# Tile 4's mask and eviction, two bank copies and four loads take other places in their engines' queues

## The chip, the cores and the metric

One core of a Trainium2 chip runs the whole kernel. The metric is the device time of one execution in microseconds (us). The kernel before takes 1176.93 us, the median of 3 runs (1176.62 to 1178.44).

## The reference

A transformer block with modulation, over 1024 tokens of width 512: a layernorm scaled and shifted, causal attention (32 query heads of size 128, which share 8 key and value heads, with rotary embedding), a gated residual, a second layernorm, and a dense layer with a low-rank part whose rank a router chooses per token. All in float32.

```python
q = (x @ wq).reshape(B, T, H, HD).transpose(0, 2, 1, 3)
k = (x @ wk).reshape(B, T, KV, HD).transpose(0, 2, 1, 3)
v = (x @ wv).reshape(B, T, KV, HD).transpose(0, 2, 1, 3)
q = q * cos + _rotate_half(q) * sin
k = k * cos + _rotate_half(k) * sin
...
scores = jnp.where(mask, scores, -jnp.inf)
att = jax.nn.softmax(scores, axis=-1)
out = jnp.einsum('bhts,bhsd->bhtd', att, v)
out = out.transpose(0, 2, 1, 3).reshape(B, T, H * HD)
return out @ wo
...
x = x + ga * _L0_attn_ref(h, L0_attn_wq, L0_attn_wk, L0_attn_wv, L0_attn_wo)
h = _layernorm(x, axis=-1) * (1 + cb) + sb
x = x + gb * _L0_ffn_ref(h, L0_ffn_W, L0_ffn_b, L0_ffn_A, L0_ffn_B, L0_ffn_gate_w, L0_ffn_gate_b)
```

## The kernel before, in words

Every float32 operand of a matmul is split into a high and a low part, and each product is three matmuls (high by high, high by low, low by high). ScalarE (ACT) writes the high part as a copy, VectorE (DVE) the low part as a subtraction: `split_hi` and `split_lo` for weights, `transposed_hi` and `transposed_lo` for probabilities, `rotated_hi` and `rotated_lo` for q and k, `output_hi` and `output_lo` for the attention output, `early_hi` and `early_lo` for the early probabilities (`pa_hi`, `pa_lo`).

The work runs over 8 groups of 4 heads (R = 4, one key and value head per group). A head is a `front` and a `back`, and every engine has its own list of both, written out by hand; semaphores tie the lists together. The next group's q, k and v are projected in the `back` of head 3, and the output projection of the group before (`wo`, tiles 0 to 7) lies in heads 0 and 1 of the next one. Which projection lies where is in `fillers(h, place, first)`: places 1 to 5 of a head, on TensorE (PE) and in the queues of the engines that evict it.

The scores of a head are 8 row tiles. Tile i has 128(i+1) keys. `masked` (DVE) adds the mask and takes the maximum, `exp` is ACT's, `inverse` (DVE) is the reciprocal of the row sum, `normalise` is GpSimd's (POOL). Tiles 0 to 3 are turned by DVE (`turn`), go to DRAM as `p_rows` and come back as `pa_lo` (`turn_columns`, SyncE's queue); tiles 4 to 7 are transposed on PE (L602) into 2 banks named `transposed`, and evicted as `pb_hi` (ACT) and `pb_lo` (DVE). PE may write a bank again once the subtraction of its last content is done. Two banks named `accumulators` hold projections and the products with v (`pva` for tokens 0 to 511, `pvb` for the rest): a bank is free when `a_taken` counts its eviction, which for q and k is `times_cos` (DVE, behind ACT's `swap_halves`, L926 and L927), for v `copy_values`. Then POOL's `rotate` multiplies by the sine (L1536) and adds (L1540).

Weights come over SyncE's queue into `stage`, which has 2 slots used in turn. A load waits until the weight two numbers before it has been split by DVE (`w_lo`); `w_number` gives each weight its number and so its slot. The `wo` weights are scaled on POOL (`scale_wo`, L1546) before their split. In the last group the weight W of the dense layer is loaded into `trig`, the table of the rotary embedding, once the last q has been rotated.

Of the kernel before, what the change touches and what calls it, by code (L numbers as in the profile page):

```python
# [22 lines left out]
P = 128  # L23
# [5 lines left out]
GROUPS = KV_HEADS  # L29
# [243 lines left out]
def adaln_block(nc, x, wq, wk, wv, wo, ffn_w, ffn_b, ffn_a, ffn_bb, gate_w, gate_b, c, wmod, out):  # L273
# [7 lines left out]
    with ExitStack() as ctx:  # L281
# [150 lines left out]
        W_GROUP = [("q", 1), ("q", 2), ("wo", 0), ("q", 3), ("wo", 1), ("wo", 2), ("wo", 3)]  # L432
        W_NEXT = [("q", 0), ("k", 0), ("v", 0)]
        W_PER = len(W_GROUP) + len(W_NEXT)

        def w_number(what, at, ahead=0):

            if what in W_GROUP:
                base = len(W_FIRST) + W_GROUP.index(what) + 1 + W_PER * (at.g + ahead)
            elif at.g + ahead == 0:  # L440
                base = W_FIRST.index(what) + 1
            else:
                base = len(W_FIRST) + len(W_GROUP) + W_NEXT.index(what) + 1 + W_PER * (at.g + ahead - 1)
# [37 lines left out]
        def _(sp):  # L481
# [58 lines left out]
            for g in range(GROUPS):  # L540
# [19 lines left out]
            sp.wait_ge(r_sum, N.value("r", ("q", (3, 1)), G7))  # L560
            sp.wait_ge(a_taken, N.value("a", ("q", (3, 1)), G7))
            sp.dma_start(fw_in, ffn_w.rearrange("(o p) i -> p o i", p=P)).then_inc(f_in, 16)
# [325 lines left out]
        def _(act):  # L888
# [74 lines left out]
            def front(h, at):  # L963
# [16 lines left out]
                else:  # L980
                    split_hi(("wo", 3), at)
# [93 lines left out]
            exp(3, 4, G7)  # L1075
            weight_hi(("W", 0), fw_hi[:, 0, :])
            exp(3, 5, G7)
# [69 lines left out]
        def _(dve):  # L1147
# [155 lines left out]
            def front(h, at):  # L1303
                hb, ahead = before(h, at)
                masked(h, 0, at)
# [358 lines left out]
```

## Time and profile before

| | |
|---|---|
| median of 3 runs | 1176.93 us |
| the profiled execution's own time | 1176.61 us |
| its span (first to last instruction) | 1174.8 us |
| mean granted TensorE clock, share of full | 0.987 |
| PE busy | 1059.3 us (90%) |
| PE weight loads busy | 875.7 us (75%) |
| DVE busy | 782.9 us (67%) |
| ACT busy | 633.2 us (54%) |
| POOL busy | 513.5 us (44%) |
| DMA, mean | 68 GB/s |

The busy times are of one execution, 1.8 us of which lie outside the span. PE is the engine that is nearly always busy, and the difference between its busy time and the span, 115.5 us, is what its idle stretches add up to. The views that follow give each such stretch with the instruction that ended it. The low part of v's weight, which stands once in each group, starts at 36.1 us and for the eighth time at 951.1; in the middle of the kernel one group follows the other after some 133 us, and head 2 takes some 23 of them.

### The profile page before, as it was taken

The page shows a single profiled execution, that of the slowest core. Times are in us where ns is not written, and L with a number is a line of the kernel's source. Part 1 is how long each engine was busy: PE and PEld are TensorE (multiplying, and loading weights), DVE is VectorE, ACT ScalarE, POOL GpSimd, SP SyncE. Part 2 cuts the span into 40 slices and gives each one's busy share as a digit, 9 for nine tenths or more (in the row PEclk, how much of TensorE's full clock was granted, in tenths as well). Part 3 has the DMA queues.
Part 4 walks back from the last instruction along what each step waited for, and adds up shares of the span by engine and source line. Part 5 has one row for each costly group of instructions (what it writes and reads, how often), then busy time and mean ns, then how long its engine had stood idle before and what let it go on. Part 6 is the DMA issues. An engine that isn't in the chain of part 4 may idle for free.

```text
span 1174.8 us, 16608 instructions
## 1 busy us (share of the span) xinstructions
PE 1059.3 (90%) x5480; PEld 875.7 (75%) x5480; DVE 782.9 (67%) x1842; ACT 633.2 (54%) x1306; POOL 513.5 (44%) x506
## 2 busy tenths in 40 slices
PE   6999889998999889998999989998999989994898
PEld 3678778786878778786878768786878768784776
DVE  4668765686558765587548766587548856584576
ACT  6446753575346753476337754476337654473443
POOL 2525642465225642356225543356325643353234
PEclk8999999999999999999999999999999999997999
DMA  6352301222102401223102311123102311123001
GB/s 216 119 179 95 104 19 54 63 73 81 54 1 73 120 24 55 63 64 90 54 1 69 111 38 54 50 77 90 55 1 63 104 49 55 46 80 99 1 19 55
DMA packets 61118, 79.84 MB, mean 68 GB/s; under 512 B 5669, under 2 KB 46757, under 8 KB 60905
## 3 DMA queue, kind: packets, MB, share of 16 engines
q1 hardware_dynamic: 61032, 78.77, 21.9%
q8 instruction: 45, 0.74, 0.3%
q14 instruction: 41, 0.33, 0.1%
HBM read 55.69 MB, written 23.07 MB: 67 GB/s over the span
## 4 chain that ended last, share of the span: by engine, by line
PE 67%; ACT 12%; DVE 11%; issue 5%; POOL 2%; DMA 2%; SPq 1%; POOLq 0%; DVEq 0%; ACTq 0%
PE accumulators L629 18%; PE accumulators L659 15%; PE accumulators L644 15%; PE scores L589 9%; PE transposed L602 6%; ACT qr L927 2%; ACT qr L926 2%; DVE p_large L1169 2%; ACT p_large L892 2%; DVE pb_lo L1181 2%; ACT pb_hi L900 2%; PE scores L857 2%; DVE turned L1193 2%; POOL qc L1540 1%; ACT o_hi L917 1%
## 5 line engine op out<-in xcount | busy, mean ns | idle before, releaser
L1527 POOL TENSOR_SCALAR p_large<-p_large,rowinv 128x640 f32<-128x640 f32 (+3 forms) x128 | 125.8, 983 | 243.5 <-DVE rowinv L1174 243.5
L1181 DVE TENSOR_TENSOR pb_lo<-transposed,pb_hi 128x512 fp32r<-128x512 f32 (+3 forms) x256 | 138.7, 583 | 104.5 <-ACT pb_hi L900 104.5
L1536 POOL TENSOR_TENSOR qr<-qr,trig 128x512 f32<-128x512 f32 x80 | 103.4, 1293 | 229.9 <-ACT qr L927 229.9
L892 ACT ACTIVATE p_large<-p_large,negmax 128x640 f32<-128x640 f32 (+3 forms) x128 | 126.5, 988 | 140.0 <-DVE negmax L1169 140.0
L900 ACT ACTIVATE pb_hi<-transposed 128x512 fp32r<-128x512 f32 (+3 forms) x256 | 117.5, 510 | 145.5 <-PE transposed L602 143.8
L602 PE MATMUL transposed<-ident,p_large 128*128 128x128 f32 x832 | 114.3, 276 | 36.3 <-DVE pb_lo L1181 29.6
L589 PE MATMUL scores<-k_hi,q_hi 128*128 128x512 f32 (+2 forms) x384 | 140.6, 366 | 0.0
L602 PEld LDWEIGHTS transposed<-ident,p_large 128*128 128x128 f32 x832 | 95.5, 141 | 60.2 <-issue 39.3
L1540 POOL TENSOR_TENSOR qc<-qc,qr 128x512 f32<-128x512 f32 x80 | 108.6, 1358 | 63.3 <-DVE qc L1223 60.7
L1169 DVE CUSTOM_DVE_ANT_0 p_large<-scores,mask 128x640 f32<-128x640 f32 (+3 forms) x128 | 128.2, 1010 | 5.8 <-PE scores L589 4.5
L589 PE MATMUL scores<-k_hi,q_lo 128*128 128x512 f32 (+2 forms) x384 | 132.0, 344 | 0.0
L589 PE MATMUL scores<-k_lo,q_hi 128*128 128x512 f32 (+2 forms) x384 | 131.5, 342 | 0.0
L1527 POOL TENSOR_SCALAR p_small<-p_small,rowinv 128x128 f32<-128x128 f32 (+3 forms) x128 | 97.4, 779 | 62.9 <-DVE rowinv L1174 62.5
L926 ACT ACTIVATE qr<-accumulators 64x512 f32<-64x512 f32 x80 | 47.7, 596 | 111.1 <-PE accumulators L644 109.7
L1248 DVE TENSOR_TENSOR y<-accumulators,y 128x512 f32<-128x512 f32 x64 | 44.1, 689 | 86.8 <-PE accumulators L659 86.8
L659 PE MATMUL accumulators<-wo_hi,o_hi 128*128 128x512 f32 x256 | 70.6, 397 | 11.1 <-DVE qc L1223 9.2
L644 PE MATMUL accumulators<-h_hi,wq_hi 128*128 128x512 f32 x256 | 70.0, 395 | 11.6 <-DVE wq_lo L1260 11.2
L589 PEld LDWEIGHTS scores<-k_hi,q_lo 128*128 128x128 f32 x384 | 72.6, 189 | 6.9
L1223 DVE TENSOR_TENSOR qc<-accumulators,trig 128x512 f32<-128x512 f32 x80 | 54.9, 686 | 34.1 <-ACT qr L927 34.0
L589 PEld LDWEIGHTS scores<-k_hi,q_hi 128*128 128x128 f32 x384 | 72.8, 190 | 5.9 <-issue 0.9
L589 PEld LDWEIGHTS scores<-k_lo,q_hi 128*128 128x128 f32 x384 | 73.2, 191 | 5.1
L1169 DVE CUSTOM_DVE_ANT_0 p_small<-scores,mask 128x128 f32<-128x128 f32 (+3 forms) x128 | 61.7, 486 | 20.6 <-PE scores L589 19.0
(167 smaller groups left out, 2278.2 us busy)
## 6 DMA issues: line engine op xcount, KB each, us to landing
p_rows<-turned SPq DMA_DIRECT2D x32, 640.0 KB, 2.9
pa_lo<-p_rows SPq DMA_DIRECT2D x128, 160.0 KB, 3.2
stage<-in_L_attn_wq_dram SPq DMA_DIRECT2D x32, 256.0 KB, 2.8
stage<-in_L_attn_wo_dram SPq DMA_DIRECT2D x32, 256.0 KB, 3.5
y<-in_L_wmod_dram SPq DMA_DIRECT2D x4, 512.0 KB, 5.7
stage<-in_L_attn_wk_dram SPq DMA_DIRECT2D x8, 256.0 KB, 2.8
stage<-in_L_attn_wv_dram SPq DMA_DIRECT2D x8, 256.0 KB, 3.8
y<-in_L_wmod_dram SPq DMA_DIRECT2D x1, 2048.0 KB, 10.6
```

Source lines behind the costliest of these rows:

```text
L589: mm = nc.tensor.matmul(S_flat[:, c0 + key:c0 + key + n], a[:, i * P:(i + 1) * P], b[:, key:key + n], start=(k == 0), stop=(k == 2))
L602: mm = nc.tensor.transpose(TB[:, b, (j % 4) * P:(j % 4 + 1) * P], row(i)[:, j * P:(j + 1) * P], ident[:])
L629: mm = nc.tensor.matmul(acc[:, c0:HALF], v[:, j, :], pt, start=(hi and v is v_hi and j == 0), stop=(not hi and j == 4 * half + 3))
L644: mm = nc.tensor.matmul(acc, a[:, k, :], b[:, k, half * HALF:(half + 1) * HALF], start=(n == 0), stop=(n == 3 * KC - 1))
L659: mm = nc.tensor.matmul(acc, a[:, r, t * P:(t + 1) * P], b[:, r, :], start=(n == 0), stop=(n == 3 * R - 1))
L892: nc.scalar.activation(row(i), row(i), ACT.Exp, bias=negmax[:, i:i + 1], scale=-1.0, accum_out=rowsum[:, i:i + 1]).then_inc(s_exp, 1)
L900: nc.scalar.activation(pt_of(i, part, True), src, ACT.Copy).then_inc(t_hi, 1)
L1169: nc.vector.tensor_tensor_reduce(row(i), S_flat[:, c0:c0 + n], mask[:, T - n:T], -SCALE, 3.4e38, ALU.add, ALU.min, negmax[:, i:i + 1]).the ...
L1181: nc.vector.tensor_tensor(pt_of(i, part, False), src, f32(pt_of(i, part, True)), ALU.subtract).then_inc(t_lo, 1)
L1527: nc.gpsimd.tensor_scalar(row(i), row(i), rowinv[:, i:i + 1], 1.0, ALU.mult, ALU.mult).then_inc(s_norm, 1)
L1536: nc.gpsimd.tensor_tensor(qr[:, s, :], qr[:, s, :], trig[:, 1, half * HALF:(half + 1) * HALF], ALU.mult).then_inc(r_sin, 1)
L1540: nc.gpsimd.tensor_tensor(qc[:, s, :], qc[:, s, :], qr[:, s, :], ALU.add).then_inc(r_sum, 1)
```

## The change

No operation is added or taken away; PE's list is the same row by row. The lists of the other four queues are:

- `masked(h, 4)` (DVE) goes from the start of `back` to the end of `front`, ahead of `turn` of tile 3.
- `transposed_hi` of tile 4 (ACT) goes ahead of the `swap_halves` of place 4.
- The `wo` 0 and `wo` 1 splits go behind that.
- The last bank copy of a head's place 5 (`times_cos` of q, or `copy_values` of the second half of v) goes ahead of masks 0 and 1 of the next `front` (DVE).
- The split of the next group's first q goes from the `back` of head 3 to its `front`, and takes the place of the split of `wo` 3; that one, with its scaling, goes into the `back`, behind tile 4's eviction. Their loads and numbers change places too.
- The split of v goes ahead of the early probabilities.
- The load of W goes ahead of the last head's `turn_columns`.

```diff
-        W_GROUP = [("q", 1), ("q", 2), ("wo", 0), ("q", 3), ("wo", 1), ("wo", 2), ("wo", 3)]
-        W_NEXT = [("q", 0), ("k", 0), ("v", 0)]
+        W_GROUP = [("q", 1), ("q", 2), ("wo", 0), ("q", 3), ("wo", 1), ("wo", 2)]
+        W_LATE = [("q", 0), ("wo", 3), ("k", 0), ("v", 0)]
...
@@ SyncE
                 turn_columns(R * g + 2)
-                load(("wo", 3), at)
                 if g + 1 < GROUPS:
                     load(("q", 0), at, 1)
+                    load(("wo", 3), at)
                     load(("k", 0), at, 1)
+                else:
+                    load(("wo", 3), at)
+                    sp.wait_ge(r_sum, N.value("r", ("q", (3, 1)), G7))
+                    sp.wait_ge(a_taken, N.value("a", ("q", (3, 1)), G7))
+                    sp.dma_start(fw_in, ffn_w.rearrange("(o p) i -> p o i", p=P)).then_inc(f_in, 16)
                 turn_columns(R * g + 3)
...
@@ ScalarE: front, then back
-                else:
-                    split_hi(("wo", 3), at)
+                elif at.g + 1 < GROUPS:
+                    split_hi(("q", 0), at, 1)
...
-                if last:
-                    split_hi(("q", 0), at, 1)
                 exp(h, 4, at)
                 exp(h, 5, at)
+                transposed_hi(h, 4, at)
+                fill(h, 4, at)
                 if h == 1:
                     split_hi(("wo", 0), at)
                 if h == 2:
                     split_hi(("wo", 1), at)
-                fill(h, 4, at)
-                transposed_hi(h, 4, at)
                 if last:
+                    split_hi(("wo", 3), at)
                     split_hi(("k", 0), at, 1)
                 exp(h, 6, at)
                 transposed_hi(h, 5, at)
                 rotated_hi(("q", ((h + 1) % R, 0)), at, int(last))
+                if last:
+                    split_hi(("v", 0), at, 1)
                 early_hi(h, at)
...
-                fill(h, 5, at, slice(0, 1) if last else slice(0, -1))
-                if last:
-                    split_hi(("v", 0), at, 1)
-                    fill(h, 5, at, slice(1, -1))
+                fill(h, 5, at, slice(0, -1))
...
@@ VectorE: front, then back
+                if h or not at.first:
+                    fill(hb, 5, at, slice(-1, None), -ahead)
                 masked(h, 0, at)
                 masked(h, 1, at)
                 if h or not at.first:
-                    fill(hb, 5, at, slice(-1, None), -ahead)
                     output_lo(hb, 0, at, ahead)
...
+                masked(h, 4, at)
                 turn(h, at, 3)
...
-                masked(h, 4, at)
                 fill(h, 2, at)
-                if last:
-                    split_lo(("q", 0), at, 1)
                 masked(h, 5, at)
...
                 fill(h, 4, at, slice(-1, None))
+                if h == 1:
+                    split_lo(("wo", 0), at)
+                if h == 2:
+                    split_lo(("wo", 1), at)
                 if last:
+                    split_lo(("wo", 3), at)
                     split_lo(("k", 0), at, 1)
...
@@ GpSimd: from front to back
-                if h == R - 1:
-                    scale_wo(3, at)
                 normalise(h, 0, at)
...
                 normalise(h, 5, at)
                 if h == 2:
                     scale_wo(2, at)
+                if last:
+                    scale_wo(3, at)
                 rotate(("q", ((h + 1) % R, 0)), at, int(last))
...
@@ the last head (tail), VectorE
-            masked(3, 4, G7)
-            weight_lo(("W", 0), 1, fw_hi[:, 0, :], fw_lo[:, 0, :])
             inverse(3, 4, G7)
             masked(3, 5, G7)
+            inverse(3, 5, G7)
+            split_lo(("wo", 3), G7)
+            weight_lo(("W", 0), 1, fw_hi[:, 0, :], fw_lo[:, 0, :])
             weight_lo(("W", 1), 2, fw_hi[:, 1, :], fw_lo[:, 1, :])
-            inverse(3, 5, G7)
             transposed_lo(3, 4, G7)
```

ScalarE in the `back` of a head 3, from the exponentials of tiles 4 and 5 to the split of k's weight, before: L926 and L927 are `swap_halves`, L900 is `transposed_hi`.

```order
L892 ACTIVATE p_large,rowsum<-p_large,negmax 128x640
L892 ACTIVATE p_large,rowsum<-p_large,negmax 128x768
L926 ACTIVATE qr<-accumulators 64x512
L927 ACTIVATE qr<-accumulators 64x512
L900 ACTIVATE pb_hi<-transposed 128x4x128
L900 ACTIVATE pb_hi<-transposed 128x128
L956 ACTIVATE wk_hi<-stage 128x512
```

The same stretch after:

```order
L896 ACTIVATE p_large,rowsum<-p_large,negmax 128x640
L896 ACTIVATE p_large,rowsum<-p_large,negmax 128x768
L904 ACTIVATE pb_hi<-transposed 128x4x128
L904 ACTIVATE pb_hi<-transposed 128x128
L930 ACTIVATE qr<-accumulators 64x512
L931 ACTIVATE qr<-accumulators 64x512
L960 ACTIVATE wo_hi<-stage 128x512
L960 ACTIVATE wk_hi<-stage 128x512
```

Tile 4's two evictions stand ahead of the swap, and `wo` 3's split has come in behind it.

ScalarE a little further on in the same head, from the evictions of tile 5 on, before: `q_hi` is `rotated_hi`, `pa_hi` is `early_hi`, the row with 1024 columns is the exponential of tile 7.

```order
L900 ACTIVATE pb_hi<-transposed 128x4x128
L900 ACTIVATE pb_hi<-transposed 128x2x128
L935 ACTIVATE q_hi<-qc 128x512
L906 ACTIVATE pa_hi<-pa_lo 128x4x320
L892 ACTIVATE p_large,rowsum<-p_large,negmax 128x1024
L926 ACTIVATE qr<-accumulators 64x512
L927 ACTIVATE qr<-accumulators 64x512
L956 ACTIVATE wv_hi<-stage 128x512
```

The same stretch after:

```order
L904 ACTIVATE pb_hi<-transposed 128x4x128
L904 ACTIVATE pb_hi<-transposed 128x2x128
L939 ACTIVATE q_hi<-qc 128x512
L960 ACTIVATE wv_hi<-stage 128x512
L910 ACTIVATE pa_hi<-pa_lo 128x4x320
L896 ACTIVATE p_large,rowsum<-p_large,negmax 128x1024
L930 ACTIVATE qr<-accumulators 64x512
L931 ACTIVATE qr<-accumulators 64x512
```

The split of v's weight stands ahead of `pa_hi`, of tile 7's exponential and of k's swap, where it stood behind them.

SyncE's loads from the `wo` 1 and 2 weights of a group to v of the next one, before:

```order
L506 DMA stage<-in_L_attn_wo_dram 128x512 x2
L513 DMA p_rows<-turned 128x1280
L519 DMA pa_lo<-p_rows 32x4x320 x4
L506 DMA stage<-in_L_attn_wo_dram 128x512
L506 DMA stage<-in_L_attn_wq_dram 128x4x128
L506 DMA stage<-in_L_attn_wk_dram 128x4x128
L513 DMA p_rows<-turned 128x1280
L519 DMA pa_lo<-p_rows 32x4x320 x4
L506 DMA stage<-in_L_attn_wv_dram 128x4x128
```

The same after:

```order
L508 DMA stage<-in_L_attn_wo_dram 128x512 x2
L515 DMA p_rows<-turned 128x1280
L521 DMA pa_lo<-p_rows 32x4x320 x4
L508 DMA stage<-in_L_attn_wq_dram 128x4x128
L508 DMA stage<-in_L_attn_wo_dram 128x512
L508 DMA stage<-in_L_attn_wk_dram 128x4x128
L515 DMA p_rows<-turned 128x1280
L521 DMA pa_lo<-p_rows 32x4x320 x4
L508 DMA stage<-in_L_attn_wv_dram 128x4x128
```

The loads of the first q and of `wo` 3 change places; v's load stands where it stood, but by its number it waits for the split of `wo` 3 and no longer for that of q.

## Rows read from the trace of the kernel before

**Rows 1.** The page's chain that ended last, whole span: share by engine.
```profile
PE 67%; ACT 12%; DVE 11%; issue 5%; POOL 2%; DMA 2%; SPq 1%; POOLq 0%; DVEq 0%; ACTq 0%
```

**Rows 2.** TensorE's waits: who, for whom, us in total, times, longest.
```profile
PE transposed L602 <- DVE pb_lo L1181: 29.6, 31, 1.0
PE accumulators L644 <- DVE wv_lo L1260: 13.9, 7, 2.0
PE accumulators L789 <- DMA trig<-in_L_ffn_W_dram: 13.3, 1, 13.3
PE accumulators L644 <- DVE wq_lo L1260: 11.2, 7, 1.6
PE accumulators L644 <- DVE vt L1239: 9.3, 7, 1.5
PE accumulators L659 <- DVE qc L1223: 9.2, 7, 1.3
PE transposed L602 <- POOL p_large L1527: 6.7, 17, 1.6
...
PE accumulators L644 <- DVE wk_lo L1260: 1.2, 7, 0.2
```

**Rows 3.** Timeline of TensorE, 640 to 690: start, us, operation, idle before.
```profile
649.93 0.77 PE L602 MATMUL transposed<-ident,p_large 128*128 128x128 f32 x5 [0.31 <-POOL p_large L1527]
...
652.89 0.84 PE L602 MATMUL transposed<-ident,p_large 128*128 128x128 f32 x6 [0.98 <-DVE pb_lo L1181]
...
671.60 1.16 PE L644 MATMUL accumulators<-h_hi,wq_hi 128*128 128x512 f32 x4 [1.60 <-DVE wq_lo L1260]
...
687.40 1.16 PE L644 MATMUL accumulators<-h_hi,wv_hi 128*128 128x512 f32 x4 [1.99 <-DVE wv_lo L1260]
```

**Rows 4.** Timeline of ScalarE, 650 to 685.
```profile
651.42 0.77 ACT L900 ACTIVATE pb_hi<-transposed 128x512 fp32r<-128x512 f32 x2
...
681.29 1.26 ACT L906 ACTIVATE pa_hi<-pa_lo 128x1280 fp32r<-128x1280 f32 x1
...
682.45 1.14 ACT L892 ACTIVATE p_large<-p_large,negmax 128x1024 f32<-128x1024 f32 x1
...
683.71 0.60 ACT L926 ACTIVATE qr<-accumulators 64x512 f32<-64x512 f32 x1
```

**Rows 5.** Timeline of VectorE, 650 to 687.
```profile
652.05 0.89 DVE L1181 TENSOR_TENSOR pb_lo<-transposed,pb_hi 128x512 fp32r<-128x512 f32 x2 [0.55 <-ACT pb_hi L900]
...
678.90 0.68 DVE L1260 TENSOR_TENSOR wk_lo<-stage,wk_hi 128x512 fp32r<-128x512 f32 x1
...
685.59 1.67 DVE L1260 TENSOR_TENSOR wv_lo<-stage,wv_hi 128x512 fp32r<-128x512 f32 x1
```

**Rows 6.** GpSimd: timeline at 685, and line 1546 (min/median/max ns).
```profile
685.44 1.27 POOL L1536 TENSOR_TENSOR qr<-qr,trig 128x512 f32<-128x512 f32 x1
...
L1546 POOL TENSOR_TENSOR stage<-stage,ga_b x32: 1286/1298/1718, 90.5 to 1062.7; 128x512 f32<-128x512 f32 x32
```

**Rows 7.** SyncE's issue at 674, its landing; all loads into stage (min/median/max).
```profile
674.93 0.43 SPq L506 DMA_DIRECT2D stage<-in_L_attn_wv_dram  x1
...
stage<-in_L_attn_wv_dram SPq DMA_DIRECT2D x1, 256.0 KB, 3.7
...
DMA to landing us min/median/max: 2.5/2.9/10.5
```

**Rows 8.** The tail: timelines of TensorE and GpSimd, and the W load's landing.
```profile
1081.74 1.97 PE L789 MATMUL accumulators<-ident,trig 128*128 128x128 f32 x8 [13.33 <-DMA trig<-in_L_ffn_W_dram]
...
1099.24 1.20 PE L659 MATMUL accumulators<-wo_hi,o_hi 128*128 128x512 f32 x4 [1.96 <-DVE o_lo L1215]
...
1061.45 1.29 POOL L1540 TENSOR_TENSOR qc<-qc,qr 128x512 f32<-128x512 f32 x1
...
trig<-in_L_ffn_W_dram SPq DMA_DIRECT2D x1, 1024.0 KB, 8.2
```

**Rows 9.** Busy by stretch: PE, PEld, DVE, ACT, POOL, PEclk, DMA share, GB/s.
```profile
1080.00:1090.00 10.00, 6.63 (x31) 5.85 (x32) 4.04 (x9) 3.35 (x8) 1.71 (x2) 0.56 0.12 40
```

More of the change, by code:

```diff
@@ L431, in adaln_block @@
         W_FIRST = [("k", 0), ("q", 0), ("v", 0)]
-        W_GROUP = [("q", 1), ("q", 2), ("wo", 0), ("q", 3), ("wo", 1), ("wo", 2), ("wo", 3)]
-        W_NEXT = [("q", 0), ("k", 0), ("v", 0)]
-        W_PER = len(W_GROUP) + len(W_NEXT)
+        W_GROUP = [("q", 1), ("q", 2), ("wo", 0), ("q", 3), ("wo", 1), ("wo", 2)]
+        W_LATE = [("q", 0), ("wo", 3), ("k", 0), ("v", 0)]
+        W_PER = len(W_GROUP) + len(W_LATE)
         def w_number(what, at, ahead=0):
@@ L439, in w_number @@
                 base = len(W_FIRST) + W_GROUP.index(what) + 1 + W_PER * (at.g + ahead)
+            elif what == ("wo", 3):
+                base = len(W_FIRST) + len(W_GROUP) + (2 if at.g + ahead < GROUPS - 1 else 1) + W_PER * (at.g + ahead)
             elif at.g + ahead == 0:
@@ L442, in w_number @@
             else:
-                base = len(W_FIRST) + len(W_GROUP) + W_NEXT.index(what) + 1 + W_PER * (at.g + ahead - 1)
+                base = len(W_FIRST) + len(W_GROUP) + W_LATE.index(what) + 1 + W_PER * (at.g + ahead - 1)
             return base if at.turn is None else base + at.turn * W_PER
@@ L552, in _ @@
                 turn_columns(R * g + 2)
-                load(("wo", 3), at)
                 if g + 1 < GROUPS:
                     load(("q", 0), at, 1)
+                    load(("wo", 3), at)
                     load(("k", 0), at, 1)
+                else:
[3 more added lines that the diff above has]
+                    sp.dma_start(fw_in, ffn_w.rearrange("(o p) i -> p o i", p=P)).then_inc(f_in, 16)
                 turn_columns(R * g + 3)
-            sp.wait_ge(r_sum, N.value("r", ("q", (3, 1)), G7))
-            sp.wait_ge(a_taken, N.value("a", ("q", (3, 1)), G7))
-            sp.dma_start(fw_in, ffn_w.rearrange("(o p) i -> p o i", p=P)).then_inc(f_in, 16)
             sp.wait_ge(w_lo, w_number(("wo", 3), G7))
@@ L1075, in _ @@
             exp(3, 4, G7)
+            exp(3, 5, G7)
+            split_hi(("wo", 3), G7)
             weight_hi(("W", 0), fw_hi[:, 0, :])
-            exp(3, 5, G7)
             weight_hi(("W", 1), fw_hi[:, 1, :])
@@ L1323, in front @@
                     split_lo(("q", h + 1), at)
-                else:
-                    split_lo(("wo", 3), at)
+                elif at.g + 1 < GROUPS:
+                    split_lo(("q", 0), at, 1)
                 turn(h, at, 0, 1, 2)
@@ L1343, in back @@
                 inverse(h, 5, at)
+                fill(h, 4, at, slice(0, -1))
+                transposed_lo(h, 4, at)
+                masked(h, 6, at)
+                fill(h, 4, at, slice(-1, None))
                 if h == 1:
@@ L1347, in back @@
                     split_lo(("wo", 1), at)
-                fill(h, 4, at, slice(0, -1))
-                transposed_lo(h, 4, at)
-                masked(h, 6, at)
-                fill(h, 4, at, slice(-1, None))
                 if last:
+                    split_lo(("wo", 3), at)
                     split_lo(("k", 0), at, 1)
@@ L1357, in back @@
                 rotated_lo(("q", ((h + 1) % R, 0)), at, int(last))
+                if last:
+                    split_lo(("v", 0), at, 1)
                 early_lo(h, at)
@@ L1361, in back @@
                     split_lo(("wo", 2), at)
-                fill(h, 5, at, slice(0, 1) if last else slice(0, -1))
-                if last:
-                    split_lo(("v", 0), at, 1)
-                    fill(h, 5, at, slice(1, -1))
+                fill(h, 5, at, slice(0, -1))
                 if last:
@@ L1567, in back @@
                     scale_wo(2, at)
+                if last:
+                    scale_wo(3, at)
                 rotate(("q", ((h + 1) % R, 0)), at, int(last))
@@ L1611, in _ @@
                 front(R - 1, at)
-            for i in range(4, 8):
+            normalise(3, 4, G7)
+            scale_wo(3, G7)
+            for i in range(5, 8):
                 normalise(3, i, G7)
```

## The prediction

> **What bounds the kernel now.** I read the chain that ended last first: 67% of it is TensorE, 12% ScalarE, 11% VectorE [rows 1]. TensorE sets the pace, its list is the same before and after, so the change can only win or lose in its waits. The table of waits comes second. The reader is to see that eight kinds make up nearly all of what TensorE waits for another engine in the attention part, and that the change touches each [rows 2]: 29.6 us for the subtraction that frees a `transposed` bank (31 times), 13.9 for v's weight, 13.3 once for W, 11.2 for the next group's q weight, 9.3 and 9.2 for a bank of `accumulators` in the fronts of heads 0 and 1 (7 times each), 6.7 for tile 4's normalisation, 1.2 for k's weight. Together 94.4 us, the ceiling of a gain from waits. Third come the timelines of one head 2 and one head 3, which show for each wait who is late and what stands behind the late one.
>
> **The `transposed` banks.** In head 2 the transposes of tile 4 start at 649.93 and those of tile 5 at 652.89, 0.98 late [rows 3]. ACT starts to evict tile 4 at 651.42 only, because the swap of q, two halves of 0.60, stands before it [rows 4]; DVE follows at 652.05 [rows 5]. The first four transposes of tile 4 are done near 650.45 (part of the 0.77 of the row), so the eviction can start about 0.97 earlier, the subtraction is done by 651.8, and TensorE comes to tile 5 at 652.89 - 0.98 = 651.91. The wait falls from 0.95 (29.6 / 31) to about 0.1. The swap ends some 0.8 later than before, but the multiplication by the cosine stands in DVE behind tile 4's subtraction and mask 6 anyway, and both come earlier. For the heads other than head 3, 24 of the 31: 24 x 0.85 = 20 us. Bounds: 12 (half of it comes back, below) to 23.
>
> **The fronts.** In heads 0 and 1 TensorE waits 9.3 / 7 = 1.3 us for a bank whose copy stands behind masks 0 and 1. Now the copy stands first. For v its source has been ready for long, for q it waits for ACT's swap, which stands behind tile 6's eviction; that swap ends before masks 0 and 1 could start. Masks 0 and 1 then begin when the copy ends, up to 0.6 later; behind them are four exponentials, which have until the products with v. 14 x 1.2 = 17 us. Bounds 8 and 18.5.
>
> **Tile 4's normalisation.** Mask 4 passes the turn of tile 3, but mask 5 does not, and the reciprocal of tile 4 stands behind mask 5, so tile 4 is ready only 0.1 earlier. In head 3 a new wait of 0.2 appears where q's projection no longer hides it. The turn goes out 0.7 later; `pa_hi` has about that much before it, because it stands behind q's rotation. I take 0, bounds -5 (0.2 in each of 24 heads) and 5 (most of the 6.7).
>
> **Head 3, 7 times.** Its waits are 1.60 for q's weight, 0.95 for the bank, 0.17 (1.2 / 7) for k and 1.99 for v, 4.7 in all [rows 2, 3]. The first two go, so TensorE is ready for k's projection 2.4 us earlier. But v's load, issued at 674.93 [rows 7], now waits for the split of `wo` 3. I add up: q's projection from 669.9 to 672.7; tile 4's eviction (0.77) until 674.2, swap (2 x 0.60) until 675.4, ACT's copy of `wo` 3 until 676.0 [rows 4]. POOL must have scaled it (1.30 [rows 6], behind tile 5's normalisation), about 675.3, not late. DVE has tile 4's subtraction (0.89), mask 6 and the cosine before it, until 676.6. There POOL's sine (1.27 [rows 6]) has begun at 675.4: v's subtraction at 685.59 took 1.67 beside that same operation, k's 0.68 beside none [rows 5], and ended 0.6 after the sine did. So `wo` 3 is split at about 676.7 + 0.6 = 677.3, and only then is v's load issued, 2.4 later than before. It took 3.7 to land behind the four column loads; all loads into `stage` have 2.5, 2.9 and 10.5 as least, median and most [rows 7]. I take 3.3: landed at 680.6. ACT comes to the copy at about 678.8 and stands still for 1.8 us, with `pa_hi`, tile 7's exponential and k's swap queued behind it. From there 0.6 (copy) + 1.2 (`pa_hi`) + 1.2 (exponential and its read) + 1.2 (swap) [rows 4] + 0.7 (k's cosine on DVE, which frees the bank for v's first half) = 685.5, against TensorE's arrival near 683.5 and the 687.40 of before [rows 3]. So the wait for v's weight becomes one for k's bank, and head 3 gains 1.9 of 4.7: 13 us. Bounds: landing after 2.5 gives 2.7 a group (19 us); after 6.5, between the median and the most, -1.3 a group (-9 us).
>
> The Trainium skill has a rule for that stretch in SBUF — State Buffer, "Who interferes with whom": a DVE instruction with two SBUF inputs and a GpSimd instruction that reads SBUF use one port pair, and whoever has it keeps it for its whole instruction. The 1.67 beside 0.68 agrees [rows 5]. By that rule alone the moved splits stand right beside POOL's rotation, which is a rival below.
>
> **The tail.** W is issued behind the last head's turn and lands 8.2 later; TensorE waits 13.33 until 1081.74 [rows 8]. The load needs the last q's rotation, whose addition runs from 1061.45 to 1062.74. It now goes out there and shares the queue with nothing until the turn at 1069. It lands between 1068 (a little over 5 us) and 1071 (the 8.2 of before), TensorE comes at 1068.4. Before, the output projection begins at 1099.24, 17.5 after W, with a granted clock of 0.56 for 1080 to 1090 [rows 8, 9], the 1.2 GHz level, behind 13 idle us. Now `wo` 3's scaling and split (1.30 + 0.61 + 0.68) stand before the eviction of W's first bank, and the loads of A and B, which use the same slots, wait for that split and land near 1079. I come to 1086.5 for the output projection: 12.7 earlier; I take 12.5, bounds 8 (A and B late) and 15.
>
> **Sum.** 20 + 17 + 0 + 13 + 12.5 = 62.5. The profiled execution took 1176.6 us; 1176.6 - 62.5 = 1114. The median of the runs is 0.3 above it: 1114.4, rounded 1114.
>
> **Rivals.**
> Nothing takes a wait's place. All of rows 2 but some 5 us goes: 1176.9 - 89 = 1088. For it: TensorE's list has no other wait near. Against: v's load is tied to a later split, and bank copies keep their latency.
>
> v's load is slow. One load into `stage` took 10.5 [rows 7]. At 6.5 the sum falls by 22: 1136. For it: the next q load is now issued right behind it and shares the DMA engines. Against: the median of 2.9.
>
> VectorE becomes the bound in heads 1 and 2. From mask 7 to the turns it has hardly a gap; where TensorE comes 1 us earlier, its chain of tile 5, q, `pa_lo`, tile 6 and masks must follow. In particular the moved `wo` splits may meet POOL's addition and wait for it, 1.3 us in 14 places (18 us). Half of the first two terms back gives 1114 + 19 = 1133. For it: the 1.67 of rows 5. Against: DVE ends the cosine some 0.2 before POOL can start the addition, so the split should go first.
>
> Slower than before: ACT stands at v's copy, with tile 7's exponential and k's swap behind it. The other terms give 49.5, so head 3 would have to lose more than 7.1 us a group beside its 4.7 of waits, that is v landing later than 3.3 + 1.9 + 7.1 = 12.3 us after its issue. The most of all loads is 10.5, which gives -5.3 a group: 1176.9 - 49.5 + 37 = 1164. At 13 us it would be 1182.
>
> **How the numbers follow.** The forecast 0.6, nothing in a wait's place 0.08, slow load 0.12, VectorE as bound 0.16, slower 0.03, and 0.01 for no change. The range reaches from 1096 (head 3 and the tail at their better ends, 1114 - 6 - 2.5, and most of tile 4's 6.7 with the fronts whole) to 1137, which takes in the third and second rivals. 0.2% is 2.4 us, about what can be told from no change. Faster 0.96, same 0.01, slower 0.03.
>
> **What would show it.** In the waits of TensorE, the 29.6 us should be under 5, the two bank waits in the fronts under 2 together, and the one for `wq_lo` gone. In head 3 the wait before v's projection should stand, some 2 us, and name k's cosine (`qc`, DVE) instead of `wv_lo`; on ACT an idle time of 1 to 2.5 us should stand before `wv_hi`, ended by the DMA; v's load should be issued right after `wo_lo`. In the tail the wait for W should be under 3 us and the clock should not fall to 0.56. I am wrong in the main if new waits before tile 6's transposes, before `pa_lo` or before tile 4's add up to more than 10 us, or if ACT never waits for v.

## The result, and the profile after

The changed kernel takes 1117.06 us (median of 4 runs, 1116.0 to 1118.8) against 1177.6 us for the kernel before in the same session: a ratio of 0.9488, interval 0.9471 to 0.9504. The forecast was 1114, the range 1096 to 1137. The profiled execution took 1118.8 us, its span is 1117.0, 57.8 less than before.

The page of the changed kernel, busy times and chain by engine:

```profile
PE 1064.2 (95%) x5480; PEld 875.7 (78%) x5480; DVE 776.2 (69%) x1842; ACT 635.5 (57%) x1306; POOL 515.9 (46%) x506
...
PE 61%; DVE 14%; ACT 9%; issue 5%; DMA 5%; POOL 3%; SPq 1%; POOLq 0%; DVEq 0%; ACTq 0%
```

TensorE is busy for 95% of the span instead of 90%: its idle time fell from 115.5 to 52.8 us, and its busy time for the same instructions rose by 4.9. The others have about the work they had. The chain has less of PE in it than before [rows 1] and 5% of DMA instead of 2%.

TensorE's waits in the changed kernel, from the view by waiter and releaser (us in total, times, longest):

```profile
PE accumulators L648 <- DVE wk_lo L1263: 14.5, 7, 2.3
...
PE transposed L606 <- DVE pb_lo L1184: 5.9, 32, 0.6
PE transposed L606 <- POOL p_large L1529: 4.6, 8, 1.5
...
PE accumulators L633 <- ACT pa_hi L910: 2.1, 4, 0.7
...
PE accumulators L648 <- DVE qc L1226: 1.2, 5, 0.3
```

Read beside [rows 2]: the bank of the transposes 29.6 to 5.9, the waits for v's and q's weights, for `vt` and for `qc` in the fronts 43.6 to nothing but the 1.2 of the last row, W's 13.3 to nothing. One is new: k's weight, 1.2 to 14.5 us, in each of the 7 groups about 2.1. `pa_hi` is new with 2.1.

TensorE in a head 3 of the changed kernel (start, us, operation, idle before), which answers to [rows 3]:

```profile
646.03 0.77 PE L606 MATMUL transposed<-ident,p_large 128*128 128x128 f32 x5 [0.43 <-POOL p_large L1529]
...
648.20 0.85 PE L606 MATMUL transposed<-ident,p_large 128*128 128x128 f32 x6 [0.18 <-DVE pb_lo L1184]
...
652.47 1.15 PE L648 MATMUL accumulators<-h_hi,wk_hi 128*128 128x512 f32 x4 [2.06 <-DVE wk_lo L1263]
...
658.50 1.20 PE L648 MATMUL accumulators<-h_hi,wv_hi 128*128 128x512 f32 x4 [0.35 <-DVE qc L1226]
```

The transposes of tile 5 wait 0.18, q's projection not at all, k's 2.06, v's 0.35 for k's cosine. With tile 4's 0.43 these sum to 3.0, against 4.7 before. Why k waits shows in the timelines of DVE, POOL, ACT and SyncE at the same place:

```profile
649.86 0.80 DVE L1263 TENSOR_TENSOR wo_lo<-stage,wo_hi 128x512 fp32r<-128x512 f32 x1
650.58 1.75 DVE L1263 TENSOR_TENSOR wk_lo<-stage,wk_hi 128x512 fp32r<-128x512 f32 x1
```

```profile
648.80 1.31 POOL L1538 TENSOR_TENSOR qr<-qr,trig 128x512 f32<-128x512 f32 x1 [0.28 <-ACT qr L931]
650.19 1.59 POOL L1542 TENSOR_TENSOR qc<-qc,qr 128x512 f32<-128x512 f32 x1
```

```profile
653.57 0.63 ACT L960 ACTIVATE wv_hi<-stage 128x512 fp32r<-128x512 f32 x1 [1.13 <-DMA stage<-in_L_attn_wv_dram]
```

```profile
650.68 0.40 SPq L508 DMA_DIRECT2D stage<-in_L_attn_wv_dram  x1
...
stage<-in_L_attn_wv_dram SPq DMA_DIRECT2D x3, 256.0 KB, 2.8
```

DVE subtracts for `wo` 3 from 649.86 to about 650.6. POOL's addition is ready since 650.19 and has its turn then: it takes 1.59 instead of 1.3. k's subtraction, next in DVE's queue, starts at 650.58 and ends at 652.3, 1.75 us for an operation that took 0.68 [rows 5]. v's load goes out at 650.68, right behind `wo` 3's subtraction, as forecast, and ACT stands still for it for 1.13 us. Over the kernel ACT waits 7.0 us for that load.

The tail of the changed kernel, TensorE, and the granted clock of one of its stretches (busy of PE, PEld, DVE, ACT, POOL, then PEclk):

```profile
1020.87 1.04 PE L793 MATMUL accumulators<-ident,trig 128*128 128x128 f32 x8
...
1023.42 0.77 PE L606 MATMUL transposed<-ident,p_large 128*128 128x128 f32 x5 [1.51 <-POOL p_large L1529]
...
1033.31 1.34 PE L633 MATMUL accumulators<-pa_hi,v_hi 128*128 128x512 f32 x4 [0.64 <-ACT pa_hi L910]
...
1039.74 1.57 PE L663 MATMUL accumulators<-wo_hi,o_hi 128*128 128x512 f32 x4 [1.96 <-DVE o_lo L1218]
```

```profile
1040.00:1050.00 10.00, 10.00 (x42) 8.15 (x42) 4.24 (x10) 1.23 (x3) 0.81 (x2) 0.83 0.01 2
```

W's transposes start at 1020.87 with no wait. From there, where the 13.33 us wait of before began (1068.4), to the output projection it is 18.9 us against 30.8 [rows 8]: 12.0 less. The stretch that follows runs partly at a lower clock (0.83 on average over these 10 us), and from the output projection to the end it is 77.3 us against 75.6.

### The profile page after: what moved, and what is told of

Its sections match the earlier page's. It is cut to its first block, busy times and chain, and to the rows that moved or that the text cites. A ratio compares the mean times of both kernels' runs of the same rounds, so it can differ in the third digit from the quotient of the medians.

```text
span 1117.0 us, 16608 instructions
## 1 busy us (share of the span) xinstructions
PE 1064.2 (95%) x5480; PEld 875.7 (78%) x5480; DVE 776.2 (69%) x1842; ACT 635.5 (57%) x1306; POOL 515.9 (46%) x506
## 4 chain that ended last, share of the span: by engine, by line
PE 61%; DVE 14%; ACT 9%; issue 5%; DMA 5%; POOL 3%; SPq 1%; POOLq 0%; DVEq 0%; ACTq 0%
PE accumulators L663 16%; PE accumulators L633 14%; PE accumulators L648 12%; PE scores L593 7%; PE transposed L606 6%; DVE p_large L1172 3%; ACT pb_hi L904 2%; DVE pb_lo L1184 2%; DVE turned L1196 2%; PE scores L861 2%; DMA pa_lo<-p_rows 2%; DMA stage<-in_L_attn_wv_dram 1%; POOL p_large L1529 1%; DMA p_rows<-turned 1%; ACT pa_hi L910 1%
## 5 line engine op out<-in xcount | busy, mean ns | idle before, releaser
L1542 POOL TENSOR_TENSOR qc<-qc,qr 128x512 f32<-128x512 f32 x80 | 113.9, 1424 | 6.8 <-DVE qc L1226 0.4
L896 ACT ACTIVATE p_small<-p_small,negmax 128x128 f32<-128x128 f32 (+3 forms) x128 | 71.0, 562 | 7.8 <-DVE negmax L1172 6.8
L663 PE MATMUL accumulators<-wo_lo,o_hi 128*128 128x512 f32 x256 | 69.4, 393 | 0.0
```

The lines of the kernel that those rows point to most:

```text
L663: mm = nc.tensor.matmul(acc, a[:, r, t * P:(t + 1) * P], b[:, r, :], start=(n == 0), stop=(n == 3 * R - 1))
L896: nc.scalar.activation(row(i), row(i), ACT.Exp, bias=negmax[:, i:i + 1], scale=-1.0, accum_out=rowsum[:, i:i + 1]).then_inc(s_exp, 1)
L1542: nc.gpsimd.tensor_tensor(qc[:, s, :], qc[:, s, :], qr[:, s, :], ALU.add).then_inc(r_sum, 1)
```

## The experiments

Every ratio is to the kernel before in the same session, so they can be compared; the changed kernel was run a second time in the third session (below). The changed kernel's two ratios are 0.9488 and 0.9491; the difference of a ratio to 0.949, times 1179 us, is the time given for an edit.

**u_t4: tile 4's eviction behind the swap again.**

```diff
 ScalarE, back
+                fill(h, 4, at)
                 transposed_hi(h, 4, at)
-                fill(h, 4, at)
```

> The changed kernel with one edit undone: ACT's swap of place 4 again stands ahead of tile 4's eviction. The account of the prediction: TensorE's wait before tile 5's transposes goes back from 5.9 us to 29.6, so the kernel takes 1117 + 20 to 24 = 1137 to 1141 us. The rival, that VectorE's chain sets the pace of a head and the early eviction only hides behind it: under half of that, 1117 to 1127, and the wait moves back without the time.

1129.62 us, ratio 0.9578 (0.955 to 0.9606): 10.4 us back. Too much for the rival, too little for the account.

```profile
PE transposed L606 <- DVE pb_lo L1184: 23.0, 32, 0.9
PE accumulators L648 <- DVE wk_lo L1263: 12.9, 7, 1.9
...
631.61 0.85 PE L606 MATMUL transposed<-ident,p_large 128*128 128x128 f32 x6 [0.65 <-DVE pb_lo L1184]
```

The wait before tile 5 comes back with 0.65 us in head 2 and not with 0.98. Head 1 has 0.66 too and so has head 3 (0.95 before); in head 0 it comes back whole (0.95).

**u_t4wo: the same, and the `wo` 0 and 1 splits ahead of both.**

```diff
 ScalarE, back
+                if h == 1: split_hi(("wo", 0), at)
+                if h == 2: split_hi(("wo", 1), at)
+                fill(h, 4, at)
                 transposed_hi(h, 4, at)
-                fill(h, 4, at)
-                if h == 1: split_hi(("wo", 0), at)
-                if h == 2: split_hi(("wo", 1), at)
 VectorE, back: the two split_lo likewise ahead of fill(h, 4, ...)
```

> The changed kernel with two edits undone: the swap of place 4 ahead of tile 4's eviction (as in u_t4), and the wo 0 and wo 1 splits ahead of both again, on ACT and DVE. u_t4 alone gave back 11 us where the account had 20 or more; its wait before tile 5 was 0.65 in heads 2 and 3 and not 0.95. Theory: the missing 0.3 belongs to the copy of wo 0 or wo 1, which delayed the swap in heads 1 and 2. Then the wait for pb_lo rises by another 3 to 5 us over 23.0 and the kernel takes 1134 to 1139. Rival: the split does nothing, the rest of the gain came from mask 4 and tile 4 being earlier, 1129 to 1131, pb_lo 23.

1136.29 us, ratio 0.9632 (0.9612 to 0.9652): 16.7 us over the changed kernel, 6.3 of them from the two splits. The wait before tile 5:

```profile
PE transposed L606 <- DVE pb_lo L1184: 31.6, 32, 1.2
...
613.32 0.85 PE L606 MATMUL transposed<-ident,p_large 128*128 128x128 f32 x6 [1.18 <-DVE pb_lo L1184]
```

ACT's copy of `wo` 0 or 1 ahead of the swap is thus worth 0.5 us of wait in heads 1 and 2 (0.66 to 1.18), more than the 0.3 that u_t4 missed: with both edits undone they wait longer than in the kernel before. Head 3, which has no such copy there, still waits 0.66 instead of 0.95. So something else in the change moves this wait too, by +0.2 in heads 1 and 2 and -0.3 in head 3; what it is was not tested.

**b_t4: this part alone, on the kernel before.** The edit is the reverse of u_t4wo.

> The kernel before with one part of the change alone: tile 4's eviction ahead of the swap, the wo 0 and wo 1 splits behind both. The account gives 31 x 0.85 = 26 us less wait for pb_lo and 20 to 24 us less time: 1153 to 1157. The rival, read from the undone edits, that TensorE's time saved there partly comes back as other waits of before (wv_lo, wq_lo, POOL): 1160 to 1166, with pb_lo under 8 and the others up by 5 or more.

1162.44 us, ratio 0.9854 (0.9837 to 0.987): 17.2 us less. The waits:

```profile
PE accumulators L644 <- DVE wv_lo L1260: 13.8, 7, 2.0
...
PE transposed L602 <- DVE pb_lo L1181: 5.3, 31, 0.2
...
PE accumulators L644 <- DVE wk_lo L1260: 2.6, 7, 0.4
...
PE 1070.1 (92%) x5480; PEld 881.0 (76%) x5480; DVE 776.2 (67%) x1842; ACT 635.5 (55%) x1306; POOL 516.7 (44%) x506
```

The time matches neither expectation fully. The wait goes down by 24.3 us and the others hardly rise (k's by 1.4), so the rival's reason is wrong although its number is nearer. What came back is in the last row: TensorE's busy time is 10.8 us more than before for the same instructions. (The two profiled executions differ by 13.0 us of span, the medians by 17.2.) The mean granted clock of this execution is 0.981 against 0.987; of its stretches of 10 us, three places between 110 us and the wait for W are under 1.00, where the kernel before had none.

How much of this is the clock can be read from the length of a group, from one first projection of k to the next:

```profile
274.71 1.16 PE L644 MATMUL accumulators<-h_hi,wk_hi 128*128 128x512 f32 x4 [0.37 <-DVE wk_lo L1260]
...
406.82 1.16 PE L644 MATMUL accumulators<-h_hi,wk_hi 128*128 128x512 f32 x4 [0.35 <-DVE wk_lo L1260]
...
537.27 1.16 PE L644 MATMUL accumulators<-h_hi,wk_hi 128*128 128x512 f32 x4 [0.37 <-DVE wk_lo L1260]
```

The first of these two groups has a lower clock near 285 and takes 132.11 us, the second has none and takes 130.45; the kernel before takes 133.1 from 413.70 to 546.81. So at the full clock 3.2 us less of this wait in a group give 2.7 us of time, and the groups with a lower clock give about 1.

**u_front: the bank copy behind masks 0 and 1 again.**

```diff
 VectorE, front
-                if h or not at.first:
-                    fill(hb, 5, at, slice(-1, None), -ahead)
                 masked(h, 0, at)
                 masked(h, 1, at)
+                if h or not at.first:
+                    fill(hb, 5, at, slice(-1, None), -ahead)
```

> The changed kernel with one edit undone: the last bank copy of place 5 stands behind masks 0 and 1 again. The account: 14 waits of 1.3 us in the fronts of heads 0 and 1 come back, 17 to 18.5 us, 1134 to 1136 us. The rival, that masks 0 and 1 and the four exponentials behind them are then earlier in all 31 fronts and give time back: 1117 to 1128.

1137.55 us, ratio 0.964 (0.9605 to 0.9675): 17.7 us back, as the account had it (17 to 18.5). Both waits are back to the digit:

```profile
PE accumulators L648 <- DVE vt L1242: 9.3, 7, 1.5
PE accumulators L663 <- DVE qc L1226: 9.2, 7, 1.3
```

**u_head3: the weight edits undone** in groups 0 to 6 (order `wo` 3, q, k, v, the splits at their old places).

```diff
-        W_LATE = [("q", 0), ("wo", 3), ("k", 0), ("v", 0)]
+        W_LATE = [("wo", 3), ("q", 0), ("k", 0), ("v", 0)]
```

> The changed kernel with the weight edits of groups 0 to 6 undone: the split of wo 3 in the front of head 3, those of the next q, k and v in the back where they stood, loads and numbers in the old order; the tail as changed. The account: head 3 gained 1.7 to 1.9 us of its waits in 7 groups, so 1117 + 12 to 14 = 1129 to 1131 us. First rival: the whole 4.7 us per head were gained, 33 us, 1150. Second rival: the weight edits gain nothing, since the wait before k took the place of those removed: 1117 within 3.

1136.57 us, ratio 0.9628 (0.9599 to 0.9658): 16.3 us back, over the account (12 to 14) but far from both rivals. The waits that stand in head 3 now:

```profile
PE accumulators L648 <- DVE wv_lo L1265: 13.7, 7, 2.0
PE accumulators L648 <- DVE wq_lo L1265: 13.4, 7, 1.9
...
PE accumulators L648 <- DVE wk_lo L1265: 2.6, 7, 0.4
```

They are 29.7 us, against 14.5 + 1.2 in the changed kernel, whose head 3 also waits 3.1 for tile 4's normalisation: 10.9 us of waits for 16.3 of time. Where no lower clock falls, a group takes 127.6 to 127.9 us against 125.9 to 126.3 in most groups of the changed kernel: 1.5 to 2 us, some 12 in 7 groups, which is the account. This execution has seven places of lower clock between 110 and 1020 us, and the rest can be theirs (last section).

**u_w: W's load behind the last columns again.**

```diff
 SyncE, last group
                     load(("wo", 3), at)
-                    sp.dma_start(fw_in, ...)
                 turn_columns(R * g + 3)
+            sp.dma_start(fw_in, ...)
```

> The changed kernel with one edit undone: the load of W goes out behind the last head's columns again, with wo 3's split where the change put it. The account: the 13 us wait for W comes back, 1127 to 1131 us, and the granted clock falls behind it. The rival, that wo 3's split in the tail costs what the early load gives: under 5 us more, 1117 to 1122.

1127.52 us, ratio 0.9562 (0.953 to 0.9594): 8.5 us back, 1127 being the account's lower end. The wait of 13.4 us is there, and the clock behind it:

```profile
PE accumulators L794 <- DMA trig<-in_L_ffn_W_dram: 13.4, 1, 13.4
```

```profile
1030.00:1040.00 10.00, 6.44 (x29) 6.05 (x30) 3.22 (x5) 2.33 (x5) 0.00 (x0) 0.53 0.38 102
```

**u_m4: mask 4 behind the turn of tile 3 again.**

```diff
 VectorE
-                masked(h, 4, at)      (end of front)
                 turn(h, at, 3)
+                masked(h, 4, at)      (start of back)
```

> The changed kernel with mask 4 behind the turn of tile 3 again. The account gave it nothing: tile 4's normalisation waits for mask 5 through the reciprocal, which does not move; 1117 within 3, with the wait for POOL (4.6 us) up by at most 2. Rival, that the early mask 4 is what keeps tile 4 ahead: 0.7 us in 24 heads, 1134. Rival the other way, that the later turn delays pa_hi: the 2.1 us of waits for pa_hi go, 1115.

1117.83 us, ratio 0.9482 (0.9458 to 0.9505): no difference. The wait for tile 4's normalisation rises from 4.6 to

```profile
PE transposed L606 <- POOL p_large L1530: 11.5, 24, 2.2
```

and TensorE's busy time is 3.1 us less. The edit is worth nothing in time, as forecast; the wait rises by more than the 2 us expected. It is 0.31 in heads 1 and 2 and 0.61 in head 3, where the changed kernel has none and 0.43: mask 4 does make tile 4 ready 0.2 to 0.3 us earlier. From the first k projection of head 3 near 147 us to the last near 905 this execution is 1.2 us longer than the changed kernel's, and from W's transposes to the end 1.2 shorter, with one place of lower clock there instead of two. Why 6.9 us of waits cost only that is not settled.

**k_first: k's split ahead of that of `wo` 3.**

```diff
-        W_LATE = [("q", 0), ("wo", 3), ("k", 0), ("v", 0)]
+        W_LATE = [("q", 0), ("k", 0), ("wo", 3), ("v", 0)]
 ScalarE and VectorE, back
-                    split(("wo", 3), at)
                     split(("k", 0), at, 1)
+                    split(("wo", 3), at)
```

> The changed kernel with k's split (copy and subtraction) ahead of that of wo 3 in the back of head 3, loads and numbers in that order; v's load then waits for k's split. Theory A, the port: k's subtraction is late because POOL's addition came between wo 3's subtraction and it; now k is ready and its wait of 14.5 us goes. Theory B, the chain behind v's load (prediction): v's projection still cannot start before k's swap, which stands behind the copy of v, pa_hi and tile 7's exponential, so the 2 us a group move from k to v's bank. A and B together: the wait for wk_lo falls under 3 us, one for qc of 10 to 15 us takes its place, time 1117 within 4. If A alone held: 1104.

1125.64 us (1118.67 to 1129.51), ratio 0.9534 (0.9495 to 0.9573), no gain and in the median a loss of 5, though one of the four runs has none. The waits, DVE's two subtractions and v's projection:

```profile
PE accumulators L648 <- DVE qc L1226: 18.2, 7, 3.8
...
PE accumulators L648 <- DVE wk_lo L1263: 2.7, 7, 0.6
...
662.64 1.21 PE L648 MATMUL accumulators<-h_hi,wv_hi 128*128 128x512 f32 x4 [2.05 <-DVE qc L1226]
```

```profile
653.94 0.78 DVE L1263 TENSOR_TENSOR wk_lo<-stage,wk_hi 128x512 fp32r<-128x512 f32 x1
654.64 1.77 DVE L1263 TENSOR_TENSOR wo_lo<-stage,wo_hi 128x512 fp32r<-128x512 f32 x1
```

Theory A holds for the waits. The second subtraction in the row is the one that POOL's addition holds up, whichever weight it is: now `wo` 3's takes 1.77 and k's 0.78. Theory B holds too, in four of the seven groups: there v's projection waits 1.7 to 2.05 us for `qc`, k's cosine, which is k's wait moved on. In the other three (near 406, 790 and 922 us) it waits 3.4 to 3.8 us, and that makes the 18.2 out of the expected 10 to 15. In these three v's load is issued right behind k's subtraction as in the others, but lands after 4.3 to 4.7 us instead of 2.5 to 2.9, and ACT stands still for it:

```profile
ACT wv_hi L960 <- DMA stage<-in_L_attn_wv_dram: 12.0, 7, 2.9
...
785.45 0.63 ACT L960 ACTIVATE wv_hi<-stage 128x512 fp32r<-128x512 f32 x1 [2.92 <-DMA stage<-in_L_attn_wv_dram]
```

In the changed kernel that row has 7.0 us, 1.1 at most. `wo` 3's late subtraction is not the reason: it stands ahead of tile 7's mask and takes as long as k's did in the changed kernel. Three groups without a late load and without a lower clock take 125.6 to 126.0 us, as in the changed kernel; those with a late load, each with a lower clock, take 130.3 and 131.7 (the third lies at the end of this count). So in those groups the order itself neither gains nor loses; the time expected (1117 within 4) was missed, as far as this trace shows, through the late loads (the prediction's second rival) and the lower clock that came with them. Why they land late is not shown, and only the slowest of the four runs was profiled.

**v_late: v's split at its old place.**

```diff
 ScalarE and VectorE, back
-                if last: split(("v", 0), at, 1)      (ahead of pa_hi, pa_lo)
+                if last: split(("v", 0), at, 1)      (behind k's swap, k's cosine)
```

> The changed kernel with v's split at its old place, behind k's swap (ACT) and k's cosine (DVE), all else as changed. ACT no longer stands still for the DMA before pa_hi. If that stand is what costs, k's bank is free 1 us earlier, and v's own subtraction becomes what v's projection waits for, beside POOL: a wait for wv_lo of about 1 us a group; 1117 within 5. If moving v's split was a real gain: 7 x 2 us more, 1131.

1121.2 us, ratio 0.9501 (0.9477 to 0.9525): within 2 us of the changed kernel, which the interval can't tell from nothing. A wait for v's subtraction appears and replaces k's cosine:

```profile
PE accumulators L648 <- DVE wk_lo L1264: 14.4, 7, 2.3
...
PE accumulators L648 <- DVE wv_lo L1264: 3.0, 7, 0.6
```

So v's earlier split alone was worth next to nothing here.

**kv_wo: the order q, k, v, `wo` 3.** v's load goes out before the group's last turn and waits for q's split alone.

```diff
-        W_LATE = [("q", 0), ("wo", 3), ("k", 0), ("v", 0)]
+        W_LATE = [("q", 0), ("k", 0), ("v", 0), ("wo", 3)]
 SyncE
-                    load(("v", 0), at)      (start of the next group)
...
                     load(("q", 0), at, 1)
-                    load(("wo", 3), at)
                     load(("k", 0), at, 1)
+                    load(("v", 0), at, 1)
                 turn_columns(R * g + 3)
+                if g + 1 < GROUPS: load(("wo", 3), at)
 GpSimd: scale_wo(3) behind normalise(h, 6)
 ScalarE and VectorE: split of wo 3 behind fill(h, 5, slice(0, -1))
```

> The changed kernel with the loads and splits in the order q, k, v, wo 3: v's load goes out before the last turn of the group, and wo 3 is scaled behind tile 6's normalisation and split behind k's and q's cosine. v's load waits for q's split alone. If the chain behind v's load sets the start of v's projection, the 7 us for which ACT waits for v's weight go, k's wait goes too, and most of head 3's 3 us of waits: 1117 - 12 to 18 = 1099 to 1105. Rival: ACT is then full in that stretch by itself, k's swap behind pa_hi and tile 7's exponential still comes late: 1110 to 1114. Second rival: wo 3's scaling and split fall on k's rotation and delay the next group's scores: slower than 1117.

1107.35 us, ratio 0.9381 (0.936 to 0.9403): 13 us less than the changed kernel, and the best of all. ACT no longer waits for v, and:

```profile
PE accumulators L649 <- DVE qc L1228: 6.9, 8, 1.7
...
PE accumulators L649 <- DVE wk_lo L1265: 2.7, 7, 0.6
...
644.91 1.16 PE L649 MATMUL accumulators<-h_hi,wk_hi 128*128 128x512 f32 x4 [0.36 <-DVE wk_lo L1265]
...
651.44 1.19 PE L649 MATMUL accumulators<-h_hi,wv_hi 128*128 128x512 f32 x4 [0.82 <-DVE qc L1228]
```

k waits 0.36 and v 0.82 (0.35 and 2.05 in k_first at the same place). It lies between the expectation (1099 to 1105) and the first rival (1110 to 1114): k's cosine still comes late.

**kv_swap: kv_wo with k's swap and cosine ahead of tile 7's exponential and reciprocal.**

```diff
 ScalarE, back of head 3
                 early_hi(h, at)
+                fill(h, 5, at, slice(0, 1))
                 exp(h, 7, at)
-                fill(h, 5, at, slice(0, -1))
+                fill(h, 5, at, slice(1, -1))
 VectorE: the same around early_lo and the reciprocal of tile 7
```

> The kernel kv_wo (loads and splits in the order q, k, v, wo 3) with one more edit: in the back of head 3, k's swap (ACT) stands behind pa_hi and ahead of tile 7's exponential, and k's cosine (DVE) behind pa_lo and ahead of the reciprocal of tile 7. kv_wo still waits 6.9 us for qc before v's projection, because k's swap stands behind that exponential. If that order is the cause the wait goes under 2 us: 1107 - 5 to 7 = 1100 to 1102. Rival: tile 7's exponential, 1.3 us later, delays its normalisation and the next front's transposes as much: 1106 to 1110.

1107.76 us, ratio 0.9392 (0.9378 to 0.9406): the same as kv_wo. The wait for `qc` falls from 6.9 to 4.6 us only, and no time is gained, as its rival said; whether tile 7 pays for it is not shown.

**after_again: the changed kernel a second time.**

> The changed kernel once more, to be compared on one chip with the others of this call: ratio to the kernel before 0.949, as measured, within 0.002. Its profile should again show no stretch of lower granted clock between 110 and 1020 us.

1118.76 us, ratio 0.9491 (0.9469 to 0.9512). The ratio repeats, the expectation on the clock does not: this execution has three places between 110 and 1020 where the granted clock of 10 us is under 1.00, the first one had none.

## Why the prediction was right, and where not

The time and its parts came out close: the parts undone one at a time give back 16.7 (`transposed` banks, with the `wo` splits), 17.7 (fronts), 16.3 (head 3), 8.5 (W) and -0.9 (mask 4), 58.3 us together, against 60.1 for the whole (0.051 x 1179). They add up within the intervals, so no large part of one edit's gain depends on another. (Each of these numbers has an interval of 2 to 4 us either way, and the tail's moved `wo` 3 split was not undone by itself.)

- *The banks of the transposes.* Forecast 20 in 24 heads and 0.95 in each head 3. The wait fell as said, to 0.18 a head instead of 0.1, but time fell by 17 only, for 31 heads. Here the size was off: the sum takes a us of wait as a us of time, and 24 to 26 us of waits gave 17 of time, undone and alone. In b_t4 a group at the full clock gives 2.7 for 3.2, and the groups with a lower clock give about 1. A step I had not split: a part of the late swap in heads 1 and 2 was the `wo` copy ahead of it.
- *The fronts.* Forecast 17, measured 17.7, and the waits are gone to nothing. That it fits to a us is in part luck: u_front has five places of lower clock, and its wait for tile 4's normalisation is 2.9 us less than the changed kernel's.
- *Tile 4's normalisation.* Forecast 0, measured 0. The new wait of 0.2 in head 3 exists, as 0.43. The step "ready only 0.1 earlier" was too small: the waits of 0.31 in heads 1 and 2 are gone, and u_m4 brings them back.
- *Head 3.* Forecast 13, measured 16.3. v's load did move behind `wo` 3's subtraction, it landed after 2.6 to 2.9 and not 3.3 us, and ACT stood for 0.9 to 1.1 and not 1.8. The step that failed is the one on TensorE's arrival: I wrote that it is ready for k's projection 2.4 us earlier and went on from there to v, without asking when k's weight is. (Its arrival "near 683.5" for v should by its own rows be 687.40 - 1.99 - 2.4 = 683.0; no term uses it.) The port rule on which I put the time of `wo` 3's subtraction applies to the next subtraction too. k then waits 2.0 to 2.3, which uses up the time that v's bank would have cost, so v waits 0.35 at most: 14.5 us for `wk_lo` and 1.2 for `qc` where I had the 14 the other way round. The sum came near all the same, by luck, because the two limits fall on nearly the same moment: at the place shown k and v wait 2.06 + 0.35 in the changed kernel, and in k_first, with k's limit removed, 0.35 + 2.05. Of the 16.3 measured some 12 can be read from groups at the full clock. This was the named rival's argument turned round: I said that the split goes before the addition, which holds for the first split in the queue and not for the second.
- *The tail.* Forecast 12.5 and W's wait under 3 us. The wait is 0, the path to the output projection 12.0 shorter, but 1.7 are lost again behind it in a stretch of lower clock, and the edit undone is worth 8.5. I had assumed that the clock would not fall once the 13 us were gone; it falls for less long, twice, at 1032 to 1038 and 1040 to 1044. W landed after 5.0 us, at the better end.
- *Tests named beforehand.* Waits before tile 5 under 5 us: 5.9. Bank waits in the fronts under 2: yes. `wq_lo` gone: yes. `qc` before v's projection: 1.2, no. ACT idle 1 to 2.5 us before `wv_hi`, ended by the DMA: 1.13 at the place shown, 0.86 to 1.13 in all, so at the lower edge. Load right behind `wo_lo`: yes. W's wait under 3: 0; the clock of 10 us not down to 0.56: 0.83. New waits of more than 10 us before tile 4, tile 6 or `pa_lo`: no, 3.1 in head 3 and 2.1 for `pa_hi`.

None of the rivals happened in whole. VectorE did not become the bound: no new wait of heads 1 and 2 is in the table. v's load was not slow in either profiled execution of the changed kernel; in k_first it was, in three of seven groups. The range's lower end of 1096 is not reached by the terms it names, which give 1099; it takes the banks' better bound of 23 as well.

## What to carry to other kernels

Where one engine is bound and waits in many short stretches, ask for each what stands ahead of the late instruction in its own queue, and move only that: here two such moves were worth 17 us each. After a move, ask of the next two instructions behind it as well when they can run, above all where two subtractions from SBUF stand in a row beside work of POOL. And the order in which a small ring of buffers is filled is a schedule: the load that everything waits for should need the earliest release, not the latest. kv_wo, which does that and has k's weight ready, is 13 us faster than the change; k_first, which has only k's weight ready, is not.

## What was not expected of the hardware

*POOL's addition comes between two subtractions of DVE.* In the changed kernel DVE has two subtractions from SBUF in a row and POOL an addition ready behind the first. The first takes 0.80, then POOL runs, then the second, 1.75 (k) or, with the order changed, 1.77 (`wo` 3). It agrees with the Trainium skill (SBUF — State Buffer, "Who interferes with whom"), where such a DVE instruction and a GpSimd read exclude each other for a whole instruction; the rows add that DVE did not keep the port for its second instruction, in none of the 7 groups.

*A wait of 2 us is sometimes followed by a lower clock.* In u_front, in the head 3 around 660, TensorE waits 2.02 us for k's weight and then finds a lower clock (busy of PE, PEld, DVE, ACT, POOL, then PEclk):

```profile
660.00:662.00 2.00, 0.74 (x4) 0.26 (x2) 2.00 (x3) 1.97 (x5) 1.92 (x2) 1.00 0.48 118
662.00:664.00 2.00, 1.25 (x3) 1.09 (x4) 2.00 (x5) 0.97 (x2) 1.07 (x2) 0.71 0.52 151
664.00:666.00 2.00, 2.00 (x6) 1.54 (x6) 2.00 (x5) 2.00 (x3) 0.00 (x0) 0.50 0.40 115
666.00:668.00 2.00, 2.00 (x10) 1.60 (x9) 1.42 (x2) 1.21 (x4) 0.38 (x1) 0.94 0.38 111
```

0.50 is the lower of the two levels, 1.2 GHz. Over the four rows (1.00 + 0.71 + 0.50 + 0.94) x 2 us leave 1.7 us of the higher level's work undone. u_front has five such places between 110 and 1020 us, u_head3 seven, b_t4 three, k_first four, the changed kernel none in one execution and three in the other.

What a place costs in time can be read from groups of one and the same execution:

| | groups with a place | groups without |
|---|---|---|
| b_t4 | 131.9, 132.1 us | 130.4 to 130.6 us |
| u_t4 | 128.6, 128.8 | 127.2 to 127.5 |
| changed kernel, second execution | 126.9, 127.0, 127.9 | 125.9 to 126.2 |

So a place costs 1 to 2 us here. It is not the whole of the scatter: the first execution of the changed kernel has a group of 127.1 without any such place, and the two executions differ by 0.5 us only. What decides is open. Nearly the same wait of 2 us stands in all 7 groups of u_front, and five of them are followed by a place; the kernel before, with waits of 1.60 and 1.99 in every head 3, had none. In k_first each of the three waits of 3.4 to 3.8 us had one, begun in the wait or right behind it, and of the four waits of 1.7 to 2.05 one. It is a likely part of the reason why parts undone or done alone differ by up to 7 us from the waits that they move; no run changed the clock alone.
